# A fused attention and mixture-of-experts kernel: the last attention step and the first 18 expert tiles written as one list per engine, with the tile tables cut into short steps

## The chip, the cores and the metric

The kernel runs on one core of one Trainium2 chip. It programs TensorE (PE), VectorE (DVE), ScalarE (ACT) and GpSimd (POOL) directly, and uses SyncE (SP) to issue transfers. Each engine works through its own list of instructions in order; semaphores are all that holds the lists together. The metric is the device time of one execution in microseconds (us), and lower is better.

## The reference

The input x has 2 batches of 2048 tokens with 128 channels. All is float32.

```
mod = silu(c) @ wmod                          # six vectors: sa, ca, ga, sb, cb, gb
h = layernorm(x) * (1 + ca) + sa
x = x + ga * linear_attention(h)              # causal, 16 heads of 8, feature map elu+1, then @ w_proj
h = layernorm(x) * (1 + cb) + sb
e = argmax(h @ Wg + bg)                       # one of 8 experts for each token
x = x + gb * (gelu(h @ W1[e]) @ W2[e])        # 128 -> 512 -> 128
```

## The kernel before

**Attention.** The 4096 tokens make 32 tiles of 128 (`NT`), taken four at a time (`GT`) in G = 8 steps, two tiles of each batch. Each engine's list is a function `step(g)`, called for g = -2 to 7. It mixes three kinds of work by hand: the core of step g (`core_scores`, `core_probs`, `core_across`, `core_within`, `core_y`, `core_proj`, `core_x1`), the front of step g+1 (`front_...`: layernorm, q, k, v, denominators), and the routing of round g-1 (`route_...`). In the last step, g = 7, there is no front left, so only the core of step 7 and the routing of round 6 fill it.

**Routing.** Round r takes the 512 tokens of step r. DVE computes the statistics (`route_stats`, `route_spread`), POOL a power (`route_root`), DVE four short steps (`route_newton`), POOL centres and scales the rows (`route_centre`, `route_scale`), and DVE modulates them (`route_modulate`, two products of 128x512). PE turns the rows (`route_turn`), ACT copies them (`route_turned`), PE makes the logits (`route_logits`), DVE the argmax (`route_argmax`, six steps), PE the ranks (`route_rank`), DVE the slots (`route_slots`, seven steps), and POOL writes the rows to their slots in DRAM, in `sorted_rows` (`route_scatter`, four indirect transfers for each round). Each expert has a region of its own in `sorted_rows`, so that its tokens fill whole tiles.

**Experts.** 39 tiles of 128 slots (`SLOT_TILES`) are computed. For tile n, SP loads the rows (`load`, `fetch`), PE turns them (`expert_turn`), ACT copies the turned rows (`column`) and the first weights (`pick_w1`), PE multiplies (`expert_up`), ACT applies GELU (`hidden`), DVE copies the second weights (`pick_w2`), PE multiplies (`expert_down`), DVE applies gate and residual (`finish`), and POOL writes the rows out (`rows_out`). Tiles 0 to 17 (RING * OPEN = 18) are unrolled, and the rest runs in loops of six tiles.

**Tables.** Which expert a tile has, and where its rows lie, is computed at run time on one partition of DVE. The first table (`early_full`, `early_table`) is made from the counts of rounds 0 to 5 and serves tiles 0 to 16 (`EARLY` = 17), which are full by then. It is emitted in `step(7)` in one piece, with `chain.link` after each operation, which makes DVE wait for that operation before it goes on:

```
                if g == G - 1:
                    early_full(chain)
                    early_table(chain)
                if front:
                    front_elu_q(g + 1)
                if core:
                    core_probs(g, 1, 0, 0)
                    core_y(g, 0)
```

The second table (`late_rest`, `late_table`) needs the counts of all rounds and serves tiles 17 to 38. Both read codes with `load_code`, which loads one word into a register.

**What SP waits for.** SP loads the rows of tiles 0 to 5 when the first table's rows are there (`early_rows`) and the scatters of rounds 0 to 5 have landed. It loads tiles 6 to 16 when the last `core_within` is done, because their buffers lie in `probs`. Then it waits for `tails_ready`, which is the first step of `route_slots(7, 3)`, writes eight blocks of zeros behind the experts' last rows (`close_runs`), waits until these, the scatters of rounds 6 and 7 and the second table are done, and loads tile 17 and the following ones.

**What holds PE at the seam.** Between the last attention step and tile 0 stand `pe.wait_ge(rden_ready, G)` and `pe.wait_ge(rank_taken, G - 1)`. The latter is given by the third step of `route_slots(6, ...)` on DVE. On DVE `first_w2` comes ahead of it: it loads three codes, and copies the second weights of tile 0.

## Time and profile before

| | us |
|---|---|
| median of 3 runs | 281.43 |
| lowest and highest | 280.58 and 283.76 |
| the profiled execution | 282.61 |
| its span, from the first to the last instruction | 280.8 |
| TensorE busy in the span | 227.6 |
| VectorE busy | 196.3 |
| ScalarE busy | 169.8 |
| GpSimd busy | 120.2 |

The profiled execution took 1.8 us more than its span. All times of the trace are counted from the start of the span. A step of attention takes some 18 us, the last one begins at 166.6 us, tile 0 starts on PE at 185.66 us, and the last tile ends at 271.9 us. In the timelines, "idle before" is the time for which the engine did nothing ahead of an instruction, with what the trace takes for the reason. "Issue" and "remote" mean that the trace shows no release.

### The profile page before, as it was taken

To read this page: it belongs to the slowest core of one execution; us is meant where nothing else is said; L and a number is where in the kernel's file an instruction comes from. 1 tells how busy PE (TensorE), PEld (TensorE's weight loads), DVE (VectorE), ACT (ScalarE), POOL (GpSimd) and SP (SyncE) were. 2 spreads that over 40 slices of the span, in tenths; PEclk is the share of its full clock that TensorE was granted. 3 is DMA by queue.
4 is the path that set the end of the run, shared out by engine and by line. 5 is a ranking of instruction groups with operands and counts; after the bars stand their busy time and mean duration, and the time that the engine had idled before them with its cause. 6 is when DMAs were issued, how large, how long until landed. Compare 5 with 4: busy or idle time off the path is not lost.

```text
span 280.8 us, 10876 instructions
## 1 busy us (share of the span) xinstructions
PE 227.6 (81%) x4167; PEld 176.4 (63%) x4167; DVE 196.3 (70%) x715; ACT 169.8 (60%) x365; POOL 120.2 (43%) x145
## 2 busy tenths in 40 slices
PE   0952998999989879899699774959796889999970
PEld 0631566566565656576466552659795789999960
DVE  3975377899878878898768799566695355545540
ACT  3269389596975776768728700526555567777720
POOL 7749700301804505408108127025555535545551
PEclk9995599999999999999979997779999999999995
DMA  6996000000210200201101102368545335444400
GB/s 188 313 352 167 2 4 5 2 2 6 78 42 26 93 6 32 88 5 60 60 4 52 67 5 88 103 176 239 157 146 198 106 117 149 136 130 140 111 13 0
DMA packets 17456, 25.75 MB, mean 92 GB/s; under 512 B 2747, under 2 KB 13117, under 8 KB 17410
## 3 DMA queue, kind: packets, MB, share of 16 engines
q1 hardware_dynamic: 13616, 16.12, 20.1%
q0 software_dynamic: 3360, 8.73, 8.7%
q8 instruction: 31, 0.51, 0.7%
q10 hardware_dynamic: 434, 0.27, 0.5%
q14 instruction: 15, 0.12, 0.1%
HBM read 14.78 MB, written 10.78 MB: 91 GB/s over the span
## 4 chain that ended last, share of the span: by engine, by line
PE 54%; DVE 19%; issue 10%; ACT 9%; another core or an unknown queue 3%; DMA 1%; POOL 1%; POOLq 1%; ACTq 0%; DVEq 0%
PE bank L1417 10%; PE bank L1408 10%; PE bank L1242 9%; DVE probs L747 4%; PE bank L1280 3%; PE bank L1183 3%; PE bank L1295 3%; ACT h_t L480 3%; DVE z_t L721 2%; PE bank L1175 2%; PE bank L1271 2%; ACT v_m L586 1%; PE bank L1401 1%; PE bank L1159 1%
## 5 line engine op out<-in xcount | busy, mean ns | idle before, releaser
L440 POOL DMA_INDIRECT out_dram<-q_m,slot_token x39 | 39.2, 1005 | 36.2 <-DVE q_m L993 19.1
L747 DVE TENSOR_TENSOR probs<-bank,causal 128x512 f32<-128x512 f32 x64 | 42.4, 683 | 13.4 <-PE bank L1242 8.5
L393 POOL TENSOR_TENSOR guess<-var,minus_half 128x4 f32<-128x4 f32 x8 | 8.3, 1039 | 99.8 <-DVE var L803 99.8
L1408 PE MATMUL bank<-q_m 128*128 128x128 f32 x312 | 42.8, 282 | 3.2 <-issue 2.9
L1242 PE MATMUL bank<-q_m,k_t 64*64 64x256 f32 x512 | 39.1, 418 | 6.6 <-issue 4.7
L1417 PE MATMUL bank<-q_m,v_m 128*128 128x128 f32 x312 | 41.8, 277 | 1.9 <-ACT v_m L586 1.9
L1408 PEld LDWEIGHTS bank<-q_m 128*128 128x128 f32 x312 | 39.3, 198 | 4.3 <-issue 4.3
L508 ACT ACTIVATE q_m<-q_t,slot_head 128x512 f32<-128x512 f32 x64 | 41.4, 710 | 0.2
L1417 PEld LDWEIGHTS bank<-q_m,v_m 128*128 128x128 f32 x312 | 37.9, 192 | 2.8 <-ACT v_m L586 2.7
L410 POOL DMA_INDIRECT sorted_rows<-row_buf,slot_i x32 | 32.1, 1004 | 8.6 <-issue 7.8
L976 DVE COPY q_m<-w_all 128x512 f32 x39 | 17.2, 444 | 20.5 <-PE bank L1417 18.2
L1242 PEld LDWEIGHTS bank<-q_m,k_t 64*64 64x64 f32 x512 | 18.5, 140 | 18.9 <-DVE probs L747 7.0
L586 ACT ACTIVATE v_m<-bank 128x512 f32<-128x512 f32 x39 | 23.2, 594 | 11.6 <-PE bank L1408 5.6
L1280 PE MATMUL bank<-probs,v_m 128*32 128x64 f32 x1024 | 24.5, 224 | 6.6 <-issue 6.0
L1280 PEld LDWEIGHTS bank<-probs,v_m 128*32 128x32 f32 x1024 | 18.3, 111 | 15.1 <-issue 14.8
L575 ACT ACTIVATE q_m<-w_all 128x512 f32 x39 | 24.4, 630 | 2.6 <-issue 2.5
L480 ACT ACTIVATE h_t<-bank,sa_col,ca_col 128x256 f32<-128x256 f32 x16 | 8.2, 560 | 25.4 <-PE bank L1175 25.4
L581 ACT ACTIVATE q_m<-bank 128x128 f32<-128x128 f32 x39 | 10.7, 276 | 20.3 <-PE bank L1401 14.1
L1271 PE MATMUL bank<-q_t,state 32*32 32x64 f32 x512 | 14.1, 226 | 4.7 <-DVE y_n L763 4.7
L540 ACT ACTIVATE h_t<-bank 128x512 f32<-128x512 f32 x8 | 4.8, 597 | 20.1 <-PE bank L1307 20.1
L522 ACT ACTIVATE v_m<-bank 64x128 f32<-64x128 f32 x64 | 13.8, 265 | 0.3
L471 ACT ACTIVATE xhat<-x_all,shift,rstd 128x128 f32<-128x128 f32 x32 | 13.1, 483 | 1.3 <-DVE shift L666 1.3
(211 smaller groups left out, 419.3 us busy)
## 6 DMA issues: line engine op xcount, KB each, us to landing
v_m<-sorted_rows SPq DMA_DIRECT2D x23, 196.0 KB
x_all<-in_L_attn_x_dram SPq DMA_DIRECT2D x16, 128.0 KB, 4.3
w_all<-in_L_ffn_W_dram SPq DMA_DIRECT2D x1, 2048.0 KB, 9.3
probs<-sorted_rows SPq DMA_DIRECT2D x10, 196.0 KB, 2.6
sorted_rows<-zeros SPq DMA_DIRECT2D x8, 196.0 KB
q_m<-sorted_rows SPq DMA_DIRECT2D x6, 196.0 KB, 2.3
out_dram<-q_m,slot_token POOLq DMA_INDIRECT x39
sorted_rows<-row_buf,slot_i POOLq DMA_INDIRECT x32
```

The lines of the kernel that those rows point to most:

```text
L410: pool.indirect_dma_start(sorted_rows, bass.IndirectOffsetOnAxis(ap=slot_i[r % 2][:, t:t + 1], axis=0), row_buf[r % 2][:, t, :], None).the ...
L440: pool.indirect_dma_start(out_rows, bass.IndirectOffsetOnAxis(ap=slot_token[ring][:], axis=0), y_row[ring], None, bounds_check=B * T - 1, ...
L508: last = nc.scalar.activation(q_m[f % 2][:, a, :], q_t[f % 2][:], ACT.Copy, scale=slot_head[:, a:a + 1])
L575: nc.scalar.activation(w1_cur[wbuf], w1_all[:, bass.ds((code >> (3 * j)) & (E - 1), 1)].rearrange("p o h -> p (o h)"), ACT.Copy).then_inc( ...
L586: nc.scalar.activation(gelu[par], up_bank[par][:].rearrange("p (k c) -> p k c", k=HC), ACT.Gelu_apprx_tanh).then_inc(gelu_ready, 1)
L747: V.tensor_tensor(probs[:, s, b, part], score_bank[part][:].rearrange("p (n t) -> p n t", n=2), causal[:].rearrange("p a t -> p (a t)").un ...
L976: V.tensor_copy(w2_cur[wbuf], w2_all[:, bass.ds((code >> (3 * j)) & (E - 1), 1)].rearrange("p o k c -> p (o k) c")).then_inc(w2c_ready, 1)
L1242: last = mm(score_bank[part][L * half:L * half + L, 4 * L * n:4 * L * n + 4 * L], k_t[par][rows, tok:tok + L], q_m[par][rows, 4 * half:4 * ...
L1271: mm(y_bank[half][rows, b * L:b * L + L], state[rows, half, b, :], q_t[par][rows, tok:tok + L], start=(b == 0), stop=False, skip_group_che ...
L1280: last = mm(y_bank[half][32 * q:32 * q + 32, b * L:b * L + L], v_m[g % 2][:, 2 * (2 * b + s) + half, a, 32 * q:32 * q + 32], probs[:, s, b ...
L1408: last = mm(up_bank[par][:, j * P:(j + 1) * P], w1_cur[wbuf][:, j * P:(j + 1) * P], h_col[par], start=True, stop=True)
L1417: last = mm(down_bank[wbuf][:, 0:C], gelu[par][:, j, :], w2_cur[wbuf][:, j, :], start=(j == 0), stop=(j == HC - 1))
```

## The change

Attention steps 0 to 6 are as before. From there to tile 17, the functions `step(7)` and the loops over tiles are replaced on PE, DVE, ACT and POOL by one flat list of calls for each engine, in a new order. SP's list is the same.

The operations of the two tables and of the last modulation become single steps, each with a wait of its own, so that other work stands between them. How many full tiles an expert has is now found by multiplying with 1/128 and rounding (adding and subtracting 1.5 * 2^23), where 256 comparisons and a sum stood before. Codes are loaded one at a time (`take_code`) instead of three in a row.

The logits and ranks of rounds 6 and 7 go to bank 0 (`F0`), so that banks 1 and 2 are free for `expert_turn`. The wait for `rank_taken` ahead of tile 0 goes away, and new waits come: `core_proj(7)` waits for `logit_taken` of round 6, `route_rank(6)` for `x1_ready` of step 7, `route_turn(7)` for `rank_taken` of round 6, and the first tiles for the banks that the last attention step still uses. Buffers of tiles move (`gelu`, `h_col`, `w2_cur`) so that they don't overlap with those of the last step. `core_sums(7, 3)`, whose result nobody read, is left out. On POOL the centring and scaling of round 6 come after all four scatters of round 5, and all four scatters of round 7 come ahead of `rows_out(6, ...)`.

```
-        gelu = [flat_v[1][:, n * HID:(n + 1) * HID].rearrange("p (k c) -> p k c", k=HC) for n in range(2)]
+        gelu = [at[:].rearrange("p (k c) -> p k c", k=HC) for at in (relu_k, exp_k)]
...
-            for g in range(G):
+            for g in range(G - 1):
                 step(g)
...
-            def early_full(chain):
-                chain.link(V.scalar_tensor_tensor(out=cnt[:], in0=place[0:1, :, GT], scalar=-float(P), in1=region[:],
-                                                  op0=ALU.add, op1=ALU.subtract))
-                chain.link(V.tensor_tensor(r_cmp[:], cnt[:].unsqueeze(2).broadcast_to([1, E, NT]), iota_tok[:],
-                                           ALU.is_ge))
-                chain.link(V.tensor_reduce(full_e[:], r_cmp[:], AX.X, ALU.add))
...
+            def made(name, instruction):
+                at[name] = len(at) + 1
+                instruction.then_inc(table_steps, 1)
+            def after(name):
+                dve.wait_ge(table_steps, at[name])
+            def early_full(part):
+                if part == 1:
+                    dve.wait_ge(slot_steps, 5 * (G - 3) + 2)
+                    made("quotient", V.scalar_tensor_tensor(out=full_e[:], in0=place[0:1, :, GT], scalar=1.0 / P,
+                                                            in1=region_down[:], op0=ALU.mult, op1=ALU.subtract))
+                if part == 2:
+                    after("quotient")
+                    made("rounded", V.tensor_scalar(full_e[:], full_e[:], ROUND, None, ALU.add))
...
-            pick_w2(1, 1, first[0], 1)
-            pick_w2(2, 2, first[0], 2)
-            early_done(chain)
...
+            core_state(G - 1, 2)
+            early_full(1)
+            core_probs(G - 1, 0, 1, 0)
+            core_probs(G - 1, 0, 1, 1)
+            early_full(2)
+            route_newton(G - 2, 1)
...
+                if g == G - 1:
+                    pe.wait_ge(logit_taken, G - 1)
...
+                if isinstance(n, int) and n < 2:
+                    pe.wait_ge(probs_ready, 1 + 8 * G + n)
...
             pe.wait_ge(rden_ready, G)
-            pe.wait_ge(rank_taken, G - 1)
-            expert_turn(0, 0, 0)
-            expert_turn(1, 1, 0)
-            expert_up(0, 0, 0)
...
+            route_turn(G - 2)
+            turn_early(0)
+            core_within(G - 1, 3)
+            route_logits(G - 2, F0)
+            turn_early(1)
+            expert_up(0, 0, 0)
+            core_proj(G - 1)
```

**VectorE, first table, in the last attention step.** Before, twelve operations of the table stand in a row (the next row is the product `probs` of L747, for which PE waits):

```order
L902 TENSOR_TENSOR r_cmp<-cnt,iota_tok 1x256
L904 TENSOR_REDUCE full_e<-r_cmp 1x8
L905 TENSOR_SCALAR tiles_e<-full_e 1x8
L906 SCALAR_TENSOR_TENSOR full_cum<-ones,full_e 1x8
L911 TENSOR_TENSOR t_cmp<-full_cum,iota_tile 1x144
L913 TENSOR_TENSOR t_skip<-t_cmp,tiles_e 1x144
L915 TENSOR_REDUCE t_exp<-t_cmp 1x18
L916 TENSOR_REDUCE t_row<-t_skip 1x18
L917 TENSOR_TENSOR digits<-t_exp,eights 1x18
L921 TENSOR_TENSOR t_row_i<-t_row,iota_tile 1x17
L923 TENSOR_REDUCE code<-digits 1x3
L925 CAST early_code<-code 1x3
```

The changed kernel at the same place; L1008 to L1017 are the full tiles, L1024 and L1029 the table, L894 to L903 the newton steps of round 6, L832 and L848 the attention products `probs` and `y_n`:

```order
L1008 TENSOR_SCALAR full_e<-full_e 1x8
L894 TENSOR_TENSOR newton<-guess 128x4
L1011 TENSOR_SCALAR full_e<-full_e 1x8
L1017 SCALAR_TENSOR_TENSOR full_cum<-ones,full_e 1x8
L897 TENSOR_TENSOR newton<-newton,var 128x4
L1024 TENSOR_TENSOR t_cmp<-full_cum,iota_tile 1x144
L848 TENSOR_TENSOR y_n<-bank,rden 128x2x64
L900 TENSOR_SCALAR newton<-newton 128x4
L1014 TENSOR_SCALAR tiles_e<-full_e 1x8
L832 TENSOR_TENSOR probs<-bank,causal 128x512
L1029 TENSOR_TENSOR t_skip<-t_cmp,tiles_e 1x144
L903 TENSOR_TENSOR rstd<-guess,newton 128x4
```

The attention products and the newton steps now stand between the table's operations, and the comparison with 256 elements is gone.

**TensorE, from the end of attention to the first tiles.** Before; L1280 is `core_within`, L1337 `route_rank(6)`, L1295 `core_proj(7)`, L1401 `expert_turn`, L1408 `expert_up`, L1417 `expert_down`:

```order
L1280 MATMUL bank6<-probs,v_m1 32x64 x16
L1280 MATMUL bank7<-probs,v_m1 32x64 x16
L1337 MATMUL bank2<-onehot,upper 32x32 x4
L1337 MATMUL bank2<-onehot,ones 32x32 x4
L1295 MATMUL bank0<-wproj_b,y_n 128x128 x4
L1401 MATMUL bank1<-ident,v_m0 128x128
L1401 MATMUL bank2<-ident,v_m0 128x128
L1408 MATMUL bank3<-q_m1,q_m0 128x128 x4
L1401 MATMUL bank1<-ident,v_m0 128x128
L1408 MATMUL bank4<-q_m1,q_m0 128x128 x4
L1417 MATMUL bank6<-q_m1,v_m1 128x128 x4
L1401 MATMUL bank2<-ident,v_m0 128x128
```

The changed kernel; L1575 is `route_turn(6)`, L1671 `expert_turn`, L1544 `core_within(7, 3)`, L1589 `route_logits(6)`, L1680 `expert_up`, L1561 `core_proj(7)`, L1693 `expert_down`:

```order
L1575 MATMUL bank0<-ident,row_buf0 128x128 x4
L1671 MATMUL bank1<-ident,v_m0 128x128
L1544 MATMUL bank7<-probs,v_m1 32x64 x16
L1589 MATMUL bank0<-wg_sb,h2_t 32x8 x16
L1671 MATMUL bank2<-ident,v_m0 128x128
L1680 MATMUL bank3<-q_m0 128x128 x4
L1561 MATMUL bank0<-wproj_b,y_n 128x128 x4
L1671 MATMUL bank1<-ident,v_m0 128x128
L1693 MATMUL bank6<-q_m0,relu_k 128x128 x4
L1671 MATMUL bank2<-ident,v_m0 128x128
L1680 MATMUL bank4<-q_m0 128x128 x4
L1680 MATMUL bank3<-q_m0 128x128 x4
```

The turn of tile 0 has moved ahead of the last `core_within`, and the up product of tile 0 ahead of the last projection; the ranks of round 6 have moved behind the up product of tile 2.

**GpSimd, from round 5 to the first tiles.** Before; L410 is `route_scatter`, L398 and L404 `route_centre` and `route_scale`, L393 `route_root`, L440 `rows_out`:

```order
L393 TENSOR_TENSOR guess<-var,minus_half 128x4
L410 DMA sorted_rows<-row_buf,slot_i 33920x392
L398 TENSOR_TENSOR row_buf<-row_buf,mean 128x4x128
L404 TENSOR_TENSOR row_buf<-row_buf,rstd 128x4x128
L410 DMA sorted_rows<-row_buf,slot_i 33920x392 x3
L393 TENSOR_TENSOR guess<-var,minus_half 128x4
L410 DMA sorted_rows<-row_buf,slot_i 33920x392 x3
L440 DMA out_dram<-q_m,slot_token 4096x128
L410 DMA sorted_rows<-row_buf,slot_i 33920x392
L440 DMA out_dram<-q_m,slot_token 4096x128 x5
```

The changed kernel (L413 `route_scatter`, L401 and L407 centring and scaling, L396 `route_root`, L441 `rows_out`):

```order
L396 TENSOR_TENSOR guess<-var,minus_half 128x4
L413 DMA sorted_rows<-row_buf,slot_i 33920x392 x4
L401 TENSOR_TENSOR row_buf<-row_buf,mean 128x4x128
L407 TENSOR_TENSOR row_buf<-row_buf,rstd 128x4x128
L396 TENSOR_TENSOR guess<-var,minus_half 128x4
L441 DMA out_dram<-q_m,slot_token 4096x128 x5
L413 DMA sorted_rows<-row_buf,slot_i 33920x392 x2
L441 DMA out_dram<-q_m,slot_token 4096x128
L413 DMA sorted_rows<-row_buf,slot_i 33920x392 x6
L441 DMA out_dram<-q_m,slot_token 4096x128 x12
```

Centring and scaling of round 6 have moved behind the last three scatters of round 5, and the scatters of round 7, which stood one by one between rows going out, are together.

## Rows read from the trace of the kernel before

**Rows 1.** Busy time in a stretch: us; PE, PEld, DVE, ACT, POOL; granted clock, DMA share, GB/s.
```profile
194.90:226.00 31.10, 25.84 (x258) 24.42 (x257) 20.27 (x85) 16.47 (x36) 17.15 (x18) 1.00 0.49 158
```

**Rows 2.** Timeline of PE, attention: start us, length, line, [idle before <-releaser].
```profile
168.09 1.09 PE L1242 MATMUL bank<-q_m,k_t 64*64 64x256 f32 x16 [1.45 <-DVE probs L747]
...
174.08 0.65 PE L1271 MATMUL bank<-q_t,state 32*32 32x64 f32 x16 [4.05 <-DVE y_n L763]
174.68 1.99 PE L1242 MATMUL bank<-q_m,k_t 64*64 64x256 f32 x16
...
181.78 1.13 PE L1295 MATMUL bank<-wproj_b,y_n 128*128 128x128 f32 x8 [0.16 <-DVE y_n L763]
185.66 0.43 PE L1401 MATMUL bank<-ident,v_m 128*128 128x128 f32 x2 [2.75 <-issue]
```

**Rows 3.** Timeline of DVE: table, product behind it, end of the modulation.
```profile
168.83 1.52 DVE L902 TENSOR_TENSOR r_cmp<-cnt,iota_tok 1x256 f32<-1x256 f32 x1
...
173.14 0.69 DVE L747 TENSOR_TENSOR probs<-bank,causal 128x512 f32<-128x512 f32 x1
...
175.26 0.69 DVE L839 TENSOR_TENSOR row_buf<-row_buf,mod_bc 128x512 f32<-128x512 f32 x1
```

**Rows 4.** Timeline of DVE: first second weights, slots of round 6, tail numbers of round 7.
```profile
184.35 0.43 DVE L976 COPY q_m<-w_all 128x512 f32 x1 [2.19 <-issue]
...
185.37 0.20 DVE L884 TENSOR_TENSOR pick_row<-bank,place 128x32 f32<-128x32 f32 x1
...
205.03 0.23 DVE L883 CAST tail_i<-place 1x8 int32<-1x8 f32 x1
```

**Rows 5.** Timeline of POOL: scaling of round 6, last scatters of rounds 5 and 7.
```profile
170.14 1.11 POOL L404 TENSOR_TENSOR row_buf<-row_buf,rstd 128x512 f32<-128x512 f32 x1
...
174.00 0.96 POOL L410 DMA_INDIRECT sorted_rows<-row_buf,slot_i  x1 [0.31 <-issue]
...
216.99 1.01 POOL L410 DMA_INDIRECT sorted_rows<-row_buf,slot_i  x1 [0.30 <-issue]
```

**Rows 6.** Timeline of SP, its own queue: loads, zeros, the load of tile 17.
```profile
178.66 4.80 SPq L279 DMA_DIRECT2D v_m<-sorted_rows  x5
...
206.35 10.64 SPq L254 DMA_DIRECT2D sorted_rows<-zeros  x8
221.45 0.01 SPq L279 DMA_DIRECT2D q_m<-sorted_rows  x1
```

**Rows 7.** SP's waits, by line: ns, first and last start us.
```profile
L292 SPq EVENT_SEMAPHORE  x2: 28/28/28, 157.9 to 177.6; - x2
```

**Rows 8.** SP's row loads: from issue to landing.
```profile
DMA to landing us min/median/max: 1.4/2.3/2.6
```

**Rows 9.** Timeline of PE, the tiles.
```profile
194.87 1.06 PE L1408 MATMUL bank<-q_m 128*128 128x128 f32 x8
...
200.74 0.25 PE L1321 MATMUL bank<-wg_sb,h_t 128*32 128x8 f32 x4 [0.52 <-issue]
...
203.49 0.27 PE L1337 MATMUL bank<-onehot,upper 128*32 128x32 f32 x8
...
225.96 0.27 PE L1401 MATMUL bank<-ident,q_m 128*128 128x128 f32 x1
...
228.11 1.16 PE L1417 MATMUL bank<-q_m,v_m 128*128 128x128 f32 x8 [0.99 <-ACT v_m L586]
...
229.21 1.06 PE L1408 MATMUL bank<-q_m 128*128 128x128 f32 x8
...
269.81 2.07 PE L1417 MATMUL bank<-q_m,v_m 128*128 128x128 f32 x16
```

**Rows 10.** Timeline of ACT: idle ahead of a column.
```profile
214.30 0.28 ACT L581 ACTIVATE q_m<-bank 128x128 f32<-128x128 f32 x1 [3.10 <-remote]
```

**Rows 11.** The page: the copies of the first weights, mean ns of one.
```profile
L575 ACT ACTIVATE q_m<-w_all 128x512 f32 x39 | 24.4, 630 | 2.6 <-issue 2.5
```

**Rows 12.** DMA queues, 160 to 232 us: packets, MB, share of 16 engines.
```profile
q8 instruction: 7, 0.11, 0.7%
```

632 lines of the change are left out of this document (470 added, 162 removed).

## The prediction

> **What bounds the kernel now.** I read the timeline of TensorE first, because it is the busiest engine, and looked there for idle time. In the steady tiles there is none: the up product of tile 17 starts at 229.21 and the last two down products at 269.81 [rows 9], so 22 up and 21 down products take 40.6 us, 0.944 us each or 1.89 us a tile. The granted clock and the order of that stretch don't change. What can be won lies between 166.6 us, where the last attention step starts, and tile 17. There I see three losses.
>
> First, DVE works on the table from 168.83 to 173.14 [rows 3]. It is 4.3 us in which it does nothing for attention, and PE stands idle for 4.05 us until 174.08. Then PE runs slower: the 16 score products of 174.68 take 1.99 us, where those of 168.09 took 1.09 [rows 2]. That is the ratio of the two levels, 1.2 and 2.4 GHz, after idle time.
>
> Second, PE stands idle for 2.75 us ahead of tile 0, from 182.91 (the projection of 181.78 and its 1.13 us) to 185.66. The trace puts it down to "issue" [rows 2]. The code has a wait for `rank_taken` of round 6 there, and DVE gives it with the operation of 185.37, which ends at 185.57 [rows 4]. It was late because DVE was idle for 2.19 us ahead of 184.35, where the code has three loads of codes into registers [rows 4].
>
> Third, between 194.87 (up product 4) and 225.96 (turn of tile 17) [rows 9] PE is busy for 25.84 of 31.10 us [rows 1], so 5.3 us are idle. No semaphore explains them: within the 32 products of the logits PE stops for 0.52 us [rows 9], and ACT stands for 3.10 us ahead of a column whose input was there [rows 10]. Code is loaded by transfers (7 on one queue in this stretch [rows 12]) beside the loads of rows and zeros, and I take these idle times for late code.
>
> On the other side, I read what SP waits for. Its first row load is issued at 178.66 [rows 6], 1.06 us after its wait for the scatters ended at 177.6 [rows 7], which is 2.64 us after the last scatter of round 5 ended on POOL (174.00 and 0.96) [rows 5]. The zeros start at 206.35 and the last is issued at 216.99 [rows 6]; tile 17 is loaded at 221.45, because the last scatter of round 7 is not over on POOL before 218.00 [rows 5]. PE turns tile 17 only at 225.96, so this chain has 2 us to spare now.
>
> **The first load.** The four scatters of round 5 no longer have centring and scaling between them, 2.2 us that end at 171.25 (170.14 and 1.11) [rows 5]. The last scatter ends at 172.8, its landing lets SP go at 175.4, the load is issued at 176.5, and with 2.3 to 2.6 us to landing [rows 8] row 0 is there at 179.0. The table must be ready by 175.4. Its operations now stand between attention products, 0.5 us or less at a time, and with half a dozen such steps it ends at 172 to 173.5, so it is not what is late.
>
> **The last attention step.** The stall of 4.05 us goes, since `probs` and `y_n` no longer wait for the table. What is late next is the modulation of round 6: centring and scaling now start at 172.9 on POOL, end at 175.1, and the two products of DVE (1.4 us, the second one being that of 175.26 [rows 3]) end at 176.6, 0.65 us later than before. PE turns the rows until 177.4, and then stands at the turn of tile 0 until 179.0, with the last `core_within`, the logits, up product 0 and the projection behind it. That is a new wait of 1.6 us, and `core_within` holds back `y_n`, the projection and the loads of tiles 6 to 16. I place the projection at 181.2 to 182.3, so it gains only 0.6 us. But up product 0 is done by then, and the wait of 2.75 us is gone. PE's idle time in this step comes in pieces of 1 to 1.6 us; if the clock falls all the same, the 3 us of work from 179 to 182 take up to 1.5 us more.
>
> **Tiles 0 to 3.** The state that before has at 194.87 (four up products, three down products and the projection done) is reached when six more products, 5.7 us, and the ranks of round 6 are done, at 188.5. ACT copies first weights in 0.63 us [rows 11] and has two shorter steps for each tile, less than 1.89 in all. The gain is 6.4 us here.
>
> **Code loads and moved work.** DVE still loads its codes, some 0.7 us each (2.19 in three), now one at a time and outside what PE waits for. The rounding in place of the 256 comparisons saves DVE something under 1.5 us (the comparison took 1.52 [rows 3]) off the path. GELU's table load moves ahead of the first weights, where ACT had nothing to do. The eight products left out are some 0.3 us of PE. The extra constants on POOL at the start are hidden by transfers and not on the path. I cost these at nothing; without that cover the codes are worth 1.4 us.
>
> **Tiles 4 to 17.** From 188.5 PE has the same work left as from 194.87: 13 up and 11 down products now against 12 and 12. Busy 25.84 us, the turn of tile 17 would be due at 214.3, and with the same 5.3 us of idle time at 219.6. For this idle time both bounds are open: nothing, or as before. I take it as before, since the same code is loaded beside the same transfers.
>
> The Trainium skill (Runtime: NRT & Kernel Launch, Instruction fetch mechanics) says that the sequencer loads code in blocks of 16 KiB while it works, and that crossing into a new block is mostly hidden. By that page the idle 5.3 us would be something else, and if it were waits of one engine's order for another's, the new lists could take all of them away. The row with 0.52 us within one group of products speaks against the page here.
>
> **The rows of tile 17.** Now the chain through SP. The ranks of round 7 stand behind up product 8 and down product 6, nine products (8.5 us) and some 2.2 us of turns and routing after 188.5, so at 199.2. Before, from the ranks at 203.49 [rows 9] to the end of the tail numbers at 205.26 [rows 4] it took 1.8 us; now a `finish` stands between them, 2.2 us. That makes 201.4, or 202.9 with some of the idle time ahead of it. SP then needs 1.1 us to the first zeros, 10.64 us to the last, 2.5 us to its landing (taken as that of a load), 1.06 us to the load of tile 17 and 2.5 us for that: 17.8 us. The scatters of round 7 are now together, four at some 1.3 us (0.96 and the 0.31 ahead of it [rows 5]), so they are over some 5 us after the slots and no longer last. The turn of tile 17 comes at 219.2 to 220.7. Both chains agree, and I take 219.8.
>
> **The sum.** From 225.96 PE needs 45.9 us to the end of the last product at 271.88, 0.99 us of it idle ahead of 228.11 [rows 9], so 44.9 us. From 219.8 this gives 264.7, 7.2 us earlier; the output behind it stays. The profiled execution would go from 282.61 to 275.4, and the median, 1.2 us below it, from 281.43 to 274.2.
>
> **Rivals.** (a) *More is won.* The late code doesn't come back, because the lists place work that hides it, and zeros go out without their gap. Then the turn of tile 17 is bounded by SP, 200.7 and some 15.5 us, at 216.2: 10.8 us won, 270.6. For it speaks that PE and ACT stood together for lack of code; against it, that nothing in the change touches code or transfers. 0.15.
>
> (b) *The lists lock into each other.* They are fixed orders; a late code block of 2 to 3 us on ACT (3.10 [rows 10]) or DVE now stops more, since up product 16 stands ahead of down product 14 and turns are waited for early. Two such blocks more on the path leave 7.2 - 4.5 = 2.7 to 4 us: 278. 0.18.
>
> (c) *The change doesn't do what it says.* PE's wait for the table becomes a wait for row 0, and the late chain is held by the scatters at 221.45 as before: the turn of tile 17 at 223.9, 3.1 us won, and with the clock at half in the last step 1.5 us: 280. 0.07.
>
> (d) *Slower.* DVE bounds tiles 1 to 12. In 194.9 to 226 it was busy for 20.27 of 31.1 us [rows 1]. The list puts the last norm, the slots of two rounds and the second table, all in order, between `finish` and `pick_w2`, and PE can't be more than three tiles ahead of either. If each of the 13 tiles from 4 on took 0.8 us more for it, 10.4 us would be lost and 3.2 us more than won: 284.6. It decides from 7.2 / 13 = 0.55 us a tile on. Against it: the same work fitted before, with a third of DVE free. 0.05.
>
> The forecast has 0.55. The range reaches from (a) over the forecast, with half clock and one late code block, to (b): 270.3 to 279.4. A measurement of this kernel tells about 1% (2.8 us) from no change. Faster by over 1%: the forecast, (a) and most of (b), 0.86; within 1%: 0.09; slower: 0.05.
>
> **What would show it.** In the changed kernel's trace: no idle time over 2 us on PE between 168 and 176; PE waiting some 1.5 us ahead of the first turn, near 179; the projection near 182; down product 2 near 188; zeros from 202 or 203; the load of tile 17 near 217, and PE idle ahead of its turn. I am wrong if row 0 lands after 181, if the zeros start after 205, or if PE is idle for much over 5 us between tiles 4 and 17.

## The result, and the profile after

The changed kernel takes 288.79 us (median of 4 runs, 286.31 to 293.09) beside 281.84 us of the kernel before on the same chip: a ratio of 1.0215, interval 1.0156 to 1.0274. It is slower by 1.6 to 2.7%, where 274.2 us was forecast. Ratios and intervals here and below are taken from the fast runs of each kernel alone (293.09 us is a slow one), so they are not quite the quotients of the medians. The profiled execution took 289.83 us, with a span of 288.1. Its last products end at 279.08, where the prediction had 264.7.

The new order of PE's list does what the prediction read in it up to the first load. The timeline of PE in the last attention step, start, length and line as in [rows 2]:

```profile
169.33 0.27 PE L1523 MATMUL bank<-v_n,k_n 64*32 64x32 f32 x5 [0.16 <-issue]
170.07 0.28 PE L1523 MATMUL bank<-v_n,k_n 64*32 64x32 f32 x6 [0.47 <-issue]
...
175.35 1.98 PE L1506 MATMUL bank<-q_m,k_t 64*64 64x256 f32 x16 [2.41 <-DVE probs L832]
177.26 0.65 PE L1535 MATMUL bank<-q_t,state 32*32 32x64 f32 x16
178.99 0.65 PE L1535 MATMUL bank<-q_t,state 32*32 32x64 f32 x16 [1.08 <-DVE y_n L848]
...
184.31 1.06 PE L1561 MATMUL bank<-wproj_b,y_n 128*128 128x128 f32 x8
```

The stall of 4.05 us is gone and others stand in its place: 2.41 and 1.08 us, and stops of 0.5 us within groups of small products. The granted clock was 0.50 from 175.35 to 182.7. What DVE did in the meantime, from its timeline:

```profile
167.27 0.30 DVE L1024 TENSOR_TENSOR t_cmp<-full_cum,iota_tile 1x144 f32<-1x144 f32 x1
170.22 0.29 DVE L848 TENSOR_TENSOR y_n<-bank,rden 128x128 f32<-128x128 f32 x1 [2.65 <-remote]
...
172.44 0.69 DVE L832 TENSOR_TENSOR probs<-bank,causal 128x512 f32<-128x512 f32 x1 [1.78 <-remote]
```

The product of 170.22 needs PE's group of 166.92, which had ended at 167.57. It begins 2.65 us later, and "remote" says that the profile knows no release that fits. In these 5 us POOL issues its four scatters of round 5, at 166.60, 167.94, 169.20 and 170.47. SP's waits show what that does to the first load. The scatters had landed at 173.2, and SP then waited for the row numbers of the table, which DVE finished at 175.72 (engine and line, waited for, us in total, times, longest):

```profile
SPq L278 <- DVE t_row_i L1044: 2.5, 1, 2.5
```

The same stands, larger, in the tiles. DVE's timeline, with its idle times without release and the tail numbers:

```profile
208.63 0.19 DVE L963 COPY counts<-bank 128x32 f32<-128x32 f32 x1 [6.08 <-remote]
...
210.39 0.15 DVE L974 CAST tail_i<-place 1x8 int32<-1x8 f32 x1
...
222.06 0.43 DVE L1148 COPY q_m<-w_all 128x512 f32 x1 [5.51 <-remote]
...
226.47 0.43 DVE L1148 COPY relu_q<-w_all 128x512 f32 x1 [2.90 <-remote]
```

ACT's in the same stretch:

```profile
208.85 0.28 ACT L611 ACTIVATE q_m<-bank 128x128 f32<-128x128 f32 x1 [4.20 <-remote]
...
221.80 0.60 ACT L616 ACTIVATE relu_k<-bank 128x512 f32<-128x512 f32 x1 [6.63 <-remote]
...
226.36 0.60 ACT L616 ACTIVATE exp_k<-bank 128x512 f32<-128x512 f32 x1 [3.45 <-remote]
```

PE, where the lines to compare are [rows 9]:

```profile
203.09 0.27 PE L1607 MATMUL bank<-onehot,upper 128*32 128x32 f32 x8
...
222.45 2.08 PE L1693 MATMUL bank<-q_m,relu_k 128*128 128x128 f32 x8 [4.83 <-issue]
...
227.22 2.05 PE L1680 MATMUL bank<-q_m 128*128 128x128 f32 x8 [2.49 <-issue]
...
232.81 0.27 PE L1671 MATMUL bank<-ident,q_m 128*128 128x128 f32 x1
```

The last of them is the turn of tile 17, whose row had been loaded from 228.86 on; PE did not wait for it. From 191.4 to 232.81 PE was busy for 29.74 of 41.41 us at a granted clock of 0.84; before, as many products (258) took 25.84 of 31.10 us at 1.00 [rows 1].

POOL, whose transfers run on without a gap while the others stand (five from 201.42 to 206.52, nine from 213.09 to 223.93):

```profile
206.52 0.96 POOL L413 DMA_INDIRECT sorted_rows<-row_buf,slot_i  x1 [0.30 <-issue]
213.09 0.96 POOL L413 DMA_INDIRECT sorted_rows<-row_buf,slot_i  x1 [5.61 <-DVE slot_i L987]
214.36 1.09 POOL L413 DMA_INDIRECT sorted_rows<-row_buf,slot_i  x1 [0.30 <-issue]
...
223.93 0.98 POOL L441 DMA_INDIRECT out_dram<-q_m,slot_token  x1 [0.59 <-issue]
```

And SP's queue, beside [rows 6]:

```profile
176.72 4.82 SPq L282 DMA_DIRECT2D v_m<-sorted_rows  x5
...
211.29 15.21 SPq L257 DMA_DIRECT2D sorted_rows<-zeros  x8
228.86 0.33 SPq L282 DMA_DIRECT2D q_m<-sorted_rows  x1
```

The reader should see three things. The counts of round 7 (DVE, 208.63) had their input at 203.4 and came 5 us late. The zeros take 15.21 us and not 10.64. And the idle times of DVE and ACT end at almost the same moments (208.63 and 208.85, 222.06 and 221.80, 226.47 and 226.36): the first pair 1.2 us behind the end of the fifth of five transfers, the others towards the end of a run of nine and 1.5 us behind it.

### The profile page after: what moved, and what is told of

Read it like the earlier page. It is cut to its first block, busy times and chain, and to the rows that moved or that the text cites. A ratio compares the mean times of both kernels' runs of the same rounds, so it can differ in the third digit from the quotient of the medians.

```text
span 288.1 us, 10849 instructions
## 1 busy us (share of the span) xinstructions
PE 229.5 (80%) x4151; PEld 178.5 (62%) x4151; DVE 191.5 (66%) x715; ACT 167.4 (58%) x365; POOL 119.6 (42%) x146
## 4 chain that ended last, share of the span: by engine, by line
PE 57%; DVE 18%; issue 11%; ACT 6%; another core or an unknown queue 2%; DMA 1%; POOL 1%; POOLq 0%; DVEq 0%; ACTq 0%
PE bank L1680 13%; PE bank L1693 12%; PE bank L1506 9%; DVE probs L832 5%; PE bank L1544 4%; PE bank L1447 3%; ACT h_t L508 2%; PE bank L1671 2%; PE bank L1561 2%; DVE z_t L806 2%; PE bank L1439 2%; PE bank L1535 2%; PE bank L1423 1%; DMA c_col<-in_L_c_dram 1%
## 5 line engine op out<-in xcount | busy, mean ns | idle before, releaser
L441 POOL DMA_INDIRECT out_dram<-q_m,slot_token x39 | 39.6, 1015 | 35.8 <-DVE q_m L1165 23.7
L832 DVE TENSOR_TENSOR probs<-bank,causal 128x512 f32<-128x512 f32 x64 | 42.3, 683 | 15.8 <-PE bank L1506 8.9
L396 POOL TENSOR_TENSOR guess<-var,minus_half 128x4 f32<-128x4 f32 x8 | 8.3, 1039 | 99.5 <-DVE var L888 99.5
L1680 PE MATMUL bank<-q_m 128*128 128x128 f32 x312 | 42.7, 285 | 2.5 <-issue 2.5
L1680 PEld LDWEIGHTS bank<-q_m 128*128 128x128 f32 x312 | 39.7, 201 | 3.0 <-issue 2.9
L413 POOL DMA_INDIRECT sorted_rows<-row_buf,slot_i x32 | 31.9, 996 | 15.2 <-issue 7.7
L1544 PE MATMUL bank<-probs,v_m 128*32 128x64 f32 x1024 | 25.5, 227 | 10.1 <-issue 7.5
L1544 PEld LDWEIGHTS bank<-probs,v_m 128*32 128x32 f32 x1024 | 18.9, 113 | 18.4 <-issue 18.0
L1148 DVE COPY q_m<-w_all 128x512 f32 x26 | 11.2, 431 | 21.3 <-PE bank L1693 11.7
L616 ACT ACTIVATE relu_k<-bank 128x512 f32<-128x512 f32 x20 | 11.9, 593 | 13.8 <-remote 6.6
L1693 PE MATMUL bank<-q_m,relu_k 128*128 128x128 f32 x104 | 14.8, 288 | 4.8 <-issue 4.8
L1693 PEld LDWEIGHTS bank<-q_m,relu_k 128*128 128x128 f32 x104 | 13.5, 202 | 5.1 <-issue 5.1
L616 ACT ACTIVATE exp_k<-bank 128x512 f32<-128x512 f32 x19 | 11.3, 594 | 7.9 <-PE bank L1680 3.8
L1693 PE MATMUL bank<-q_m,exp_k 128*128 128x128 f32 x104 | 15.3, 296 | 0.0
L1693 PEld LDWEIGHTS bank<-q_m,exp_k 128*128 128x128 f32 x104 | 14.2, 211 | 0.0
```

What stands on the lines that cost most here:

```text
L413: pool.indirect_dma_start(sorted_rows, bass.IndirectOffsetOnAxis(ap=slot_i[r % 2][:, t:t + 1], axis=0), row_buf[r % 2][:, t, :], None).the ...
L441: pool.indirect_dma_start(out_rows, bass.IndirectOffsetOnAxis(ap=slot_token[ring][:], axis=0), y_row[ring], None, bounds_check=B * T - 1, ...
L616: nc.scalar.activation(gelu[par], up_bank[par][:].rearrange("p (k c) -> p k c", k=HC), ACT.Gelu_apprx_tanh).then_inc(gelu_ready, 1)
L832: V.tensor_tensor(probs[:, s, b, part], score_bank[part][:].rearrange("p (n t) -> p n t", n=2), causal[:].rearrange("p a t -> p (a t)").un ...
L1544: last = mm(y_bank[half][32 * q:32 * q + 32, b * L:b * L + L], v_m[g % 2][:, 2 * (2 * b + s) + half, a, 32 * q:32 * q + 32], probs[:, s, b ...
L1680: last = mm(up_bank[par][:, j * P:(j + 1) * P], w1_cur[wbuf][:, j * P:(j + 1) * P], h_col[par], start=True, stop=True)
```

## The theories

**Theory A**: several indirect transfers of POOL in direct succession, 1.3 us apart, hold up the other engines. The change puts more of them in a row, so it loses there more than it wins. **Theory B**: the new order loses by itself (the reciprocal root late, tail numbers behind other work, the turn of tile 17 ahead of work that is ready), and the chain through SP to tile 17 ends late.

The experiments ran on four chips, and the chips differ more than the kernels do. The kernel before took 266.03 us on one and 266.81 on another, 283.41 and 279.76 (280.02 at a later time) on two more, and 281.84 in the first comparison. Ratios are always to the kernel before, run beside it on the same chip; I call the two groups the 266 and the 280 chips. This sum is over each trace, 160 to 232 us, of the idle times ahead of an instruction that are put down to "remote":

| kernel (chip) | DVE, us | ACT, us | zeros start | load of tile 17 | ratio |
|---|---|---|---|---|---|
| before (first) | 4.12 | 8.01 | 206.35 | 221.45 | 1 |
| changed (first) | 19.63 | 14.28 | 211.29 | 228.86 | 1.0215 |
| changed (e6, 280) | 19.62 | 16.50 | 210.95 | 230.66 | 1.0174 |
| changed (e17, 280) | 17.75 | 12.16 | 207.89 | 223.35 | 1.0253 |
| changed, gaps (e18, 280) | 0.64 | 0 | 200.68 | 220.86 | 0.997 |
| changed, gaps (e15, 266) | 0 | 0 | 195.74 | 215.68 | 1.0366 |

On the 266 chips the sum is 0 for every kernel that ran there, eight in all.

## The experiments

### Rows out left out, rows out in groups, POOL's old order (266 chip)

In e1 (from the changed kernel) and e2 (from the one before) the rows of tiles 0 to 11 are not written out, so those rows of the output stay unwritten. A pow of about the length of a transfer's issue stands in each one's place:

```diff
+                if isinstance(n, int) and n < 2 * RING:
+                    nc.gpsimd.tensor_tensor(spare[:, n], minus_half[:], minus_half[:], ALU.pow)
+                    return
```

> The changed kernel, in which GpSimd does not write out the rows of tiles 0 to 11: a power of 128x4 (about 1.04 us, as long as the issue of a transfer) stands in each one's place, so those rows of the output stay unwritten. Theory A (runs of three and more indirect transfers of GpSimd, 1.3 us apart, hold up the other engines): the idle times of over 2 us without a release on DVE and ACT between 200 and 230 us go, and the time falls by 6 to 12 us, to 276 to 283. Theory B (the fixed lists lock into each other; GpSimd's transfers have no part in it): GpSimd is busy as long, the idle times stay, 286 to 290.

> The kernel before with the same edit (rows of tiles 0 to 11 not written out, a power of 128x4 in their place). Theory A: its idle times without a release (208.9 to 210.6, 211.2 to 214.3, 217.9 to 219.4) go as well, 3 to 6 us faster, 276 to 279. Theory B: within 1% of 281.8.

In the kernel before, the loop's rows out in groups of three (e3):

```diff
+                    if ring % 3 == 0:
+                        pool.wait_ge(yrow_ready, pool.to_reg(RING * k + ring + 3))
```

> The kernel before; in the loop of tiles 18 to 35 GpSimd waits until three tiles are ready and writes their rows out one right behind the other, where it did one every 1.9 us. Nothing is added, and a ring of six leaves room. Theory A: after each third transfer the other engines stall for 1 us or more; six such groups make it 4 to 12 us slower, 286 to 294, with idle time on PE in a stretch that has none. Theory B: same time within 1%.

In the changed kernel, POOL's order of the last attention step as it was (e4):

```diff
             route_scatter(G - 3, 0)
+            route_centre(G - 2)
+            route_scale(G - 2)
             route_scatter(G - 3, 1)
             route_scatter(G - 3, 2)
             route_scatter(G - 3, 3)
-            route_centre(G - 2)
-            route_scale(G - 2)
```

> The changed kernel with GpSimd's old order in the last attention step: scatter 0 of round 5, centring and scaling of round 6, scatters 1 to 3. Theory A: four transfers in a row become three, the stall of 169.6 to 172.3 us on PE shrinks, 1 to 3 us faster than the changed kernel, 284 to 287. Theory B: the first load comes 2 us later, same or up to 1 us slower than the changed kernel, 288 to 289.

Measured: e1 264.55 us, ratio 0.9865 (0.9762 to 0.9968); e2 265.05, 0.9946 (0.9905 to 0.9986); e3 271.75, 1.0114 (1.0000 to 1.0227), e4 269.67, 1.0112 (1.0036 to 1.0187). No trace has an idle time put down to "remote" in 160 to 232 us, though e1 has runs of four transfers 1.3 us apart. POOL's timeline there:

```profile
194.33 0.96 POOL L414 DMA_INDIRECT sorted_rows<-row_buf,slot_i  x1 [0.44 <-issue]
195.60 1.09 POOL L414 DMA_INDIRECT sorted_rows<-row_buf,slot_i  x1 [0.30 <-issue]
197.00 0.96 POOL L414 DMA_INDIRECT sorted_rows<-row_buf,slot_i  x1 [0.31 <-issue]
198.26 0.96 POOL L414 DMA_INDIRECT sorted_rows<-row_buf,slot_i  x1 [0.30 <-issue]
```

So theory A does not hold on this chip. What limits here is the chain through SP, as the prediction said. PE waits in e1 for the row of tile 17, and then its products run at half clock for 4 us (granted clock 0.50 from 208.55 to 212.60):

```profile
208.55 0.47 PE L1675 MATMUL bank<-ident,q_m 128*128 128x128 f32 x1 [4.27 <-DMA q_m<-sorted_rows]
```

The first turn came at 169.71 in e1 and at 178.78 in e2, 9.1 us earlier, and the last product ended at 255.5 and 256.3, 0.8 us earlier. Nearly all that PE wins ahead of tile 17 is given back there: the zeros start at 192.80 and 196.72 and the load of tile 17 at 205.91 and 208.55. In e4 scatters 1 to 3 wait for the centring. Its ratio is 2.5% above that of e1, but the two differ by both edits, so neither is priced by it.

### Copies, the table alone, a later turn of tile 17 (280 chip)

> An unchanged copy of the kernel before, for its trace on the chip of the next three runs. On the chip of the first comparison it took 281.8 us and its engines stood idle for 1 to 3 us without a release, beside runs of four and more indirect transfers of POOL (198.7, 208.9, 211.2, 217.9 us); on another chip it took 266.0 us. If those idle times are the kernel's own, they are here again whatever the time; if they are the chip's, a trace of 266 us has none and a trace of 281 us has them.

> An unchanged copy of the changed kernel. If the chip is one on which the kernel before takes 280 us, the ratio should be 1.02 again. If it is one of 266 us: theory A (the loss is idle time that only a stalling chip has, and the changed kernel puts more of POOL's transfers in a row) expects no loss there, a ratio of 0.985 to 1.0, with the zeros starting before 195 us. Theory B (the new order itself loses: rstd late, tail numbers behind other work, the turn of tile 17 ahead of work that is ready) expects 1.01 or more there too, with TensorE idle for 3 us or more ahead of the turn of tile 17.

e7 is the kernel before with its first table (the same operations, the comparison of 256 included) in nine steps between the attention products:

```diff
                     core_probs(g, 1, 0, 0)
+                    if g == G - 1:
+                        early_part(4)
                     core_y(g, 0)
+                    if g == G - 1:
+                        early_part(5)
```

> One part of the change alone: the kernel before, its first table in nine short steps between the attention products of the last step, with the same operations, the rest untouched. The prediction's first step says that TensorE's idle time of 4 us there goes and that the first load of SP comes no earlier, since it waits for the scatters: 1 to 3 us earlier at the first turn where TensorE was late, and then 1 to 3 us at the end only if the chain through SP (tail numbers, zeros, rows of tile 17) comes earlier by as much, since the tail numbers follow TensorE's tiles. Theory A or B of the changed kernel both expect 0.985 to 1.0 here. If this part is itself what loses, the ratio is over 1.01.

e8 is the changed kernel with this on PE:

```diff
-            turn_early(17)
             expert_down(14, 0, 2)
             expert_down(15, 1, 0)
+            turn_early(17)
```

> The changed kernel with the turn of tile 17 behind the down products of tiles 14 and 15 on TensorE instead of ahead of them. Theory B says that TensorE stands at the turn of tile 17 for the row to land while two down products are ready: 1.9 us of the wait are filled, so 1.5 to 2.5 us less than the changed kernel (ratio lower by 0.006 to 0.009). Theory A says that the idle time there is no wait for the row, and the time stays within 0.5 us of the changed kernel's.

Measured: e5 281.15 us in one run (before: 283.41), e6 290.10, ratio 1.0174 (1.0053 to 1.0296), e7 280.97, 0.9948 (0.9909 to 0.9987), e8 294.04, 1.0343 (1.0242 to 1.0445). The idle times without release are back in all four, at the same places, and ahead of the counts of round 7 they have the same size: 6.08 us in the first run, 6.06 in e6, 6.07 in e8. In e6 PE stands for 11.35 us ahead of the up product of 228.08 (that of tile 14), while POOL issues ten transfers from 212.75 on, and turns tile 17 at 233.18 without a wait; e8 has 11.40 us at the same product. So the later turn of tile 17 had nothing to win, and theory B failed its first test; the time is no lower than that of e6 (the intervals overlap).

The table in short steps does what the first step of the prediction said. PE, e7:

```profile
166.72 1.09 PE L1281 MATMUL bank<-q_m,k_t 64*64 64x256 f32 x16 [1.72 <-DVE probs L748]
169.18 0.43 PE L1310 MATMUL bank<-q_t,state 32*32 32x64 f32 x16 [0.52 <-DVE y_n L764]
170.76 1.09 PE L1281 MATMUL bank<-q_m,k_t 64*64 64x256 f32 x16 [1.16 <-DVE probs L748]
...
177.64 1.13 PE L1334 MATMUL bank<-wproj_b,y_n 128*128 128x128 f32 x8 [0.16 <-DVE y_n L764]
```

The wait of 4.05 us becomes 0.52, 1.16 and 0.83, the scores of 170.76 run at full clock in 1.09 us, and the projection comes 3.0 us earlier than in e5 (177.64 and 180.67). The zeros come 0.5 us earlier (204.67 and 205.14), the end by 0.5%.

### Spacing, groups in the loop, rows out left out, scatters in a row (280 chip)

e10 is the changed kernel with a pow of 1.04 us, for which nothing waits, behind each scatter of rounds 5 to 7 and each of the first 18 rows out, 30 in all:

```diff
+            def gap():
+                nc.gpsimd.tensor_tensor(spare[:, next(gaps)], minus_half[:], minus_half[:], ALU.pow)
```

> The changed kernel with an operation of POOL that nothing waits for (a pow of 128 by 4, 1.04 us on an earlier chip) behind each indirect transfer of the last three rounds of scatters and of the first 18 rows out, so that two transfers start some 2.3 us apart and not 1.3. Theory A (several of POOL's indirect transfers in direct succession hold up the other engines on a chip that stalls) expects, where the kernel before takes 280 us, that ACT's and DVE's idle times without release of 4 to 12 us between 202 and 228 go or fall below 2 us each, and the time falls from 290 to 275 to 284 although 30 us of work are added to POOL. Theory B (the order of the lists and the chain through SP) expects 290 or more. On a chip of 266 us both expect no gain.

e9 and e11 repeat e3 and e1 on this chip.

> The kernel before, its rows out in the loop of ten rounds issued in groups of three, so that three indirect transfers follow each other every 5.7 us there; tiles 0 to 17 are untouched. It cost 1.1% on a chip of 266 us, with no idle time without release. On a chip that stalls, theory A expects 1 to 2 us without release for each group, for 18 groups 15 us or more in all (ratio 1.05 or more). Theory A2, that only code which is executed for the first time is held up beside such transfers (a loop's code is there already), expects the same 1.01 as on the other chip.

> The changed kernel, rows out of tiles 0 to 11 left out (those rows of the output aren't written), a pow of 128 by 4 in the place of each. It gained 1.35% on a chip of 266 us. On a chip that stalls, theory A expects that the stalls behind the scatters of the attention steps and of round 7 stay and that those of 217 to 228 go: 6 to 11 us less than the changed kernel, ratio 0.975 to 1.0. Theory B expects 288 to 290, ratio 1.015 or more.

e12 puts one thing of the change into the kernel before:

```diff
-                if SCATTER_AT <= n < SCATTER_AT + GT:
-                    route_scatter(G - 1, n - SCATTER_AT)
+                if n == SCATTER_AT + GT - 1:
+                    for t in range(GT):
+                        route_scatter(G - 1, t)
```

> The kernel before with one thing of the change: the four scatters of round 7 in direct succession on POOL, ahead of the row out of tile 9, where it has them one ahead of each of the rows out of tiles 6 to 9. On a chip that stalls, theory A expects that the idle times of 209 to 213 become one longer one behind the four, 1 to 4 us more on the path, ratio 1.005 to 1.015. Theory B (no effect of the row itself; only the landing of the last scatter counts, and it is issued no later) expects 1.0.

Measured: e10 294.67 us, ratio 1.0555 (1.0499 to 1.0611), e9 288.09, 1.0318 (1.0267 to 1.0368), e11 278.13 beside 279.76 (no interval is given; 4 runs, 274.57 to 280.71, so its gain is known only roughly), e12 282.07, 1.0080 (1.0047 to 1.0114).

In e10 no idle time between 160 and 232 us is put down to "remote" any more, on a chip where the changed kernel has 17.75 us of them on DVE. Where e10 has no gaps, they are still there. DVE has 0.9 to 1.0 us beside the three scatters in a row of each of five attention steps. Behind the last gap, POOL has eight rows out in a row, from 249.63 to 258.74, and beside them ACT stands again:

```profile
258.23 0.60 ACT L626 ACTIVATE exp_k<-bank 128x512 f32<-128x512 f32 x1 [4.92 <-remote]
```

The forecast of its time was over 10 us too low all the same: a gap behind each of the 30 transfers fills POOL from 200 us on, the rows out come late, DVE waits 13.54 us for the landing of one and PE 11.21 us for the row of tile 17. e12 is the cleanest of the four, since only three scatters change their place, on one engine. Two lines of DVE's timeline, and POOL's:

```profile
215.23 0.29 DVE L991 TENSOR_TENSOR q_m<-bank,probs 128x128 f32<-128x128 f32 x1 [1.99 <-remote]
223.13 0.29 DVE L991 TENSOR_TENSOR q_m<-bank,probs 128x128 f32<-128x128 f32 x1 [6.81 <-remote]
```

```profile
211.70 0.99 POOL L440 DMA_INDIRECT out_dram<-q_m,slot_token  x1 [2.33 <-DVE q_m L994]
213.00 1.01 POOL L410 DMA_INDIRECT sorted_rows<-row_buf,slot_i  x1 [0.30 <-issue]
...
220.73 0.98 POOL L440 DMA_INDIRECT out_dram<-q_m,slot_token  x1 [0.30 <-issue]
```

Eight transfers in a row, and 8.8 us of DVE's idle time beside them, where e5, the kernel before on another 280 chip, has 2.06 us in that stretch. It costs 0.8%. e11 keeps the stalls beside the scatters (2.57 us of DVE, 3.83 of ACT near 209 to 213) and has none beside the rows out that are gone; by its median it is 0.6% below the kernel before, where the changed kernel was 2.5% above it on the same chip. Groups of three in the loop cost 1.1% on the 266 chip and 3.2% here, some 5.7 us more. The 15 us forecast for theory A counted 18 groups in ten rounds, but the loop has 18 tiles in three rounds, so six groups (e9's start at 238.65, 245.26, 251.88, 258.53, 265.35 and 271.91); 1 to 2 us for each would be 6 to 12 us. PE loses 3.12 us there in idle times of 0.42 to 0.77 us, against none in e3. So code that loops is held up as well, against A2, by somewhat under 1 us for each group of three.

### Gaps that POOL can afford (266 chip)

e13 is the kernel before with a pow of 1.04 us between scatters 1, 2 and 3 of each attention step and behind each scatter of rounds 6 and 7; e14 has the table in short steps too. e15 is the changed kernel with such gaps, and with the rows out of tiles 6 and 7 ahead of the scatters of round 7 and that of tile 8 in their middle. e16 is e13 with a smaller pow.

```diff
                     route_scatter(g - 2, 1)
+                    gap()
                     route_scatter(g - 2, 2)
+                    gap()
                     route_scatter(g - 2, 3)
```

> The kernel before with a pow of 128 by 4 on POOL (1.04 us, nothing waits for it) between scatters 1, 2 and 3 of each attention step and behind each of the scatters of rounds 6 and 7. Theory A (direct succession of POOL's indirect transfers holds up the other engines on a chip that takes 280 us) expects that the idle times without release of about 1 us in each of the attention steps and of 2 to 3 us between 198 and 214 go: 4 to 8 us less, ratio 0.97 to 0.985. Theory B (these idle times are in the kernel's own waits) expects 1.0 to 1.01. On a chip of 266 us both expect 1.0.

> The same with the first table in short steps too. Theory A expects 1 to 3 us less than with the gaps alone, since the table steps gained 0.5% alone: ratio 0.965 to 0.98. Theory B 0.99 to 1.0.

> The changed kernel with such a pow between scatters 1, 2 and 3 of each step and behind each scatter of rounds 6 and 7, and with the rows out of tiles 6 and 7 ahead of the scatters of round 7 and that of tile 8 between them, so that POOL is not behind as it was with a gap after every transfer. Theory A expects 8 us or more less than the changed kernel: 272 to 281, ratio 0.97 to 1.0, TensorE without an idle time of over 4 us between 200 and 230 and the zeros from 203 to 206. Theory B (fixed order, late chain through SP) expects 286 or more, ratio 1.02.

> The kernel before with gaps at the same places, but each a pow of 128 by 1, by the times of 128 by 4 and 128 by 24 (1.04 and 4.19 us) some 0.5 us. If any work between two transfers is enough, the ratio is that of the long gaps; if the spacing itself counts, the gain is half of it or less.

Measured: e13 271.66 us, ratio 1.0219 (1.0161 to 1.0277); e14 266.94, 1.0034 (0.9998 to 1.0070); e15 275.68, 1.0366 (1.0286 to 1.0445); e16 268.69, 1.0069 (1.0022 to 1.0116). This chip shows none of the idle times, so these runs tell only what a gap costs where it removes nothing: 2.2% for the long ones and 0.7% for the short ones, which took some 0.8 us each and not 0.5. The last scatter and with it the load of tile 17 come late: 213.70 in e13 and 210.79 in e3, the nearest trace of a 266 chip, with PE idle for 4.37 and 2.24 us until it has landed. Of these 2.9 us, 1.8 are there at the turn of tile 0 already (178.57 and 176.77). In e15 PE stands for 10.96 us ahead of the turn of tile 17, with the landing of its row as the releaser. With the same gaps, the table in short steps is worth 4.7 us (e14 against e13), more than the 1 to 3 expected. How much spacing is enough on a 280 chip stays open, since e16 did not run on one.

### The changed kernel with and without gaps (280 chip)

> An unchanged copy of the changed kernel. On a chip where the kernel before takes 280 us the ratio should be 1.02 again. On one of 266 us: with the rows out of tiles 0 to 11 left out it was 0.9865 and with the old order on POOL in the last attention step 1.011, so theory A (on a chip without stalls the change loses nothing) expects 0.98 to 1.0, and theory B (the order and the chain through SP lose by themselves) 1.005 to 1.015, with TensorE idle for 3 us or more ahead of the turn of tile 17 with a DMA as the releaser.

> The changed kernel with a pow on POOL between indirect transfers, as it ran before at a ratio of 1.037 on a chip without idle times without release; there it only lengthens POOL's list, and the last scatter ended at 213.2 and TensorE waited 11 us for the rows of tile 17. On a chip of 280 us theory A expects that the idle times without release of DVE and ACT are gone in this version too; by its spacing POOL still bounds tile 17, so the time should be that of the other chip's 275.7 plus what is slower there elsewhere, 280 to 288, against 286 to 290 of the changed kernel. If theory A is wrong, both keep the idle times and this version takes 295 or more.

Measured: e17 286.51 us, ratio 1.0253 (1.0198 to 1.0308); e18 279.41, 0.9970 (0.9932 to 1.0008). e18, the same text as e15, which lost 3.7% on the other chip, is 7.1 us faster here than the changed kernel. DVE's counts of round 7 and POOL's transfers ahead of them, e17:

```profile
204.67 0.96 POOL L413 DMA_INDIRECT sorted_rows<-row_buf,slot_i  x1 [0.30 <-issue]
```

```profile
205.23 0.19 DVE L963 COPY counts<-bank 128x32 f32<-128x32 f32 x1 [4.53 <-remote]
```

and e18, where POOL has a pow of 1.04 us between them:

```profile
198.92 1.04 POOL L414 TENSOR_TENSOR spare<-minus_half 128x4 f32<-128x4 f32 x1
200.16 1.03 POOL L449 DMA_INDIRECT out_dram<-q_m,slot_token  x1 [0.20 <-issue]
```

```profile
197.69 0.19 DVE L981 COPY counts<-bank 128x32 f32<-128x32 f32 x1 [0.94 <-PE bank L1625]
...
225.47 0.29 DVE L1180 TENSOR_TENSOR q_m<-bank,probs 128x128 f32<-128x128 f32 x1 [8.41 <-PE bank L1711]
```

The first load comes 3.3 us earlier (171.66 and 175.00), since the stalls of the attention steps are gone (SP waited 2.2 us for the table in e17, and not at all in e18); the counts come 7.5 us earlier, the 4.53 us above among them, and the zeros 7.2 us earlier and in 9.99 us in place of 13.20. What is left is the price of the gaps: the last scatter is issued at 217.40, the load of tile 17 at 220.86, and PE waits for it:

```profile
223.25 0.47 PE L1689 MATMUL bank<-ident,q_m 128*128 128x128 f32 x1 [8.70 <-DMA q_m<-sorted_rows]
```

This pair carries the verdict, with one reservation: e18 also has the rows out of tiles 6 to 8 earlier in POOL's list, so its gain is that of both.

The attention steps are free of that reservation, and they also show where the two groups of chips part. In steps 2 to 6 no row goes out, and all kernels have the same text there but for the gaps. POOL computes a root in each step; here are the first and the last of that stretch in e17,

```profile
68.63 1.01 POOL L396 TENSOR_TENSOR guess<-var,minus_half 128x4 f32<-128x4 f32 x1 [12.82 <-DVE var L888]
...
163.76 1.04 POOL L396 TENSOR_TENSOR guess<-var,minus_half 128x4 f32<-128x4 f32 x1 [10.26 <-DVE var L888]
```

and in e18:

```profile
70.78 1.01 POOL L397 TENSOR_TENSOR guess<-var,minus_half 128x4 f32<-128x4 f32 x1 [13.14 <-DVE var L906]
...
160.77 1.04 POOL L397 TENSOR_TENSOR guess<-var,minus_half 128x4 f32<-128x4 f32 x1 [6.48 <-DVE var L906]
```

| from the root of round 1 to that of round 6, us | 280 chip | 266 chip |
|---|---|---|
| no gaps between the scatters | 94.75 (e10) to 97.34 (before), 11 traces; 95.13 in e17 | 88.09 (e1) to 90.25 (e2), 4 traces |
| gaps between them | 89.99 (e18), 1 trace | 87.79 (e14) to 89.97 (e16), 4 traces |

From e17 to e18 the gaps save 5.1 us here, where e17 has 4.58 us of DVE put down to "remote" and e18 none; on the 266 chips they change nothing that stands clear of the spread. Without gaps the two groups of chips differ by some 7 us in this stretch, half of their 14, and with gaps hardly at all. Ahead of the first scatter they still run side by side: the root of round 1 is at 69.36 in the kernel before and at 69.31 in e3.

Theory A stands on the 280 chips. Of theory B one part is left, which the prediction had too: behind the stalls waits the chain through SP.

## Why the prediction was wrong

**The first load** came when forecast, 176.72 and 176.5, but by luck. The prediction had SP wait for the scatters until 175.4 and the table ready by then. The scatters had landed at 173.2, and the table, "not what is late", held SP for 2.5 us more. The two errors cancel. PE did not wait for row 0 but stood 2.41 and 1.08 us for DVE. **The last attention step** was wrong by 2 to 3 us (projection 184.31, not 181.2 to 182.3). The table ended at 175.99, not at 172 to 173.5, and the root was only ready at 173.41, because DVE lost 2.65 and 1.78 us beside the four scatters, which the change had moved together. Before, centring and scaling stood among them. The half clock that was held possible also came, from 175.35 to 182.7.

**Tiles 0 to 3**: the wait of 2.75 us is gone as said; the state of 188.5 is reached at 191.4 (down product 2 of 190.51), so the gain is 3.5 us and not 6.4; the missing 2.9 us are those of the step before.

**Tiles 4 to 17** is the step that failed: "with the same 5.3 us of idle time", "since the same code is loaded beside the same transfers". It was 11.7 us. I had taken the idle times of before for late code. What the runs showed in its place is that they follow POOL's runs of indirect transfers: they go when work stands between the transfers (e10, e18), go in part when the transfers go (e11), and grow when four scatters are put in a row with all code unchanged in number and order on the other engines (e12). The same transfers, put in longer rows, are not the same for the rest. The row of 0.52 us within one group, which I held against the page of the Trainium skill (Runtime: NRT & Kernel Launch, Instruction fetch mechanics), doesn't speak for late code. As much code is loaded with the stalls as without: 6 packets, 0.10 MB, on queue q8 from 160 to 232 us in e17, e18 and e15. Whether a code fetch comes late beside the transfers no run here decides.

**The rows of tile 17**: ranks of round 7 at 203.09 and not 199.2 (2.9 us of it from above); from them to the end of the tail numbers 7.5 us and not 2.2 to 3.7, by the 5.2 us that the counts stood without release; the zeros 15.21 us and not 10.64. "The scatters of round 7 are now together, four at some 1.3 us" is true in the trace, and it is the first half of the run of nine from 213.09 on. The load of tile 17 is issued at 228.86 and not at 217. PE itself stood for 4.83 and 2.49 us, and between them and behind them its clock was at half (down product 222.45 and up product 227.22, some 2 us each; granted clock 0.58 from 222.45 to 232.81). Of the 10.3 us that the stretch from 191.4 to 232.81 took more than the 31.1 us forecast, 6.4 are idle time (11.7 us and not 5.3) and 3.9 the slower clock (29.74 us busy and not 25.84). The turn of tile 17 comes at 232.81 and not at 219.8, 13.0 us late. **Behind it** PE needs 46.3 us, about as before (45.9), where I had taken the 0.99 us of idle time off. 13.0 and 1.4 are the 14.4 us between 264.7 and 279.1; with them the 274.2 of the forecast become 288.6, where the median was 288.79.

**The rivals**: (b) had the mechanism by halves, fixed orders in which one late engine stops all, but priced at two blocks of 2 to 3 us. (d), slower because DVE is too busy, had the sign right and not the cause: DVE was busy for 21.04 of the 42 us from 190 to 232. Of (a) nothing was seen, and (c) had the half clock of the last step, which was not the main loss. Of the three signs of being wrong, two came true: the zeros after 205, and PE idle for more than 5 us between tiles 4 and 17.

**Code loads and moved work** at nothing was not priced by itself. e7, with the comparison of 256 still in it, wins its 0.5%.

Open are what holds the engines up beside POOL's transfers, why two of the four chips of the experiments don't show it, and what the changed kernel itself takes on a 266 chip; its nearest relatives there were between 0.9865 (e1) and 1.0366 (e15).

## What to carry to other kernels

Idle time whose release the profile doesn't know is a term of its own: before it is taken as constant, look what runs on the other engines beside each piece of it, and whether the change moves that. A list that brings indirect transfers of POOL together can cost more than the waits that it removes, and small work put between them cost the kernel before 2.2% on a chip where nothing stalls, so a ratio wants runs on more than one chip. Of this change the table in short steps is worth keeping alone: 0.9948 (0.9909 to 0.9987) on a 280 chip, and 4.7 us on a 266 chip beside the same gaps.

## What the runs showed of the hardware

- The same kernel took 266.0 to 266.8 us on two chips and 279.8 to 283.4 on others.
- On the slower ones DVE and ACT stand without a known release beside runs of POOL's indirect transfers that are 1.3 us apart: some 1 us of DVE beside three in each of five attention steps, up to 12.31 us of ACT beside ten in e6. With 2.3 us from one to the next there was none (e10, e18; e18's 0.64 us of DVE is behind three rows out without gaps). On the other chips there was none at 1.3 us either. Five rows out 1.3 us apart from 219.71 on in e18 have none beside them; DVE waited for PE then (8.41 us).
- At the same instruction (the counts of round 7) the idle time was 6.08, 6.06 and 6.07 us on two chips and 4.53 us in e17 on a third.
- SP's eight transfers of zeros took 13.20 to 17.45 us in the four traces of the changed kernel (e8 among them), where the run of eight to ten lies beside them, and 7.91 (e12) to 10.64 us in the others.
- DVE stood idle for 2.19 us where it loads three codes into registers [rows 4], an estimate of some 0.7 us for one.
